# Attention on VectorE: the output addition of a pair of tiles placed apart from the sum of its last two blocks

## The reference, cut to what matters

```python
q, k, v = ...                         # 16 heads of 64, rotary embedding on q and k
scores  = einsum('bqhd,bkhd->bhqk', q, k) / 8
scores  = where(tril, scores, -1e9)   # causal
weights = softmax(scores)
out     = einsum('bhqk,bkhd->bqhd', weights, v)
x       = x + out.reshape(...) @ W_out
```

## Time and profile before

| | us |
|---|---|
| median of 3 runs (lowest, highest) | 2729.64 (2729.27, 2730.74) |
| the profiled execution, its own time | 2724.24 |
| its span in the trace | 2722.5 |
| PE busy / DVE busy / ACT busy | 2588.0 / 2075.0 / 1617.1 |
| mean granted TensorE clock, share of full speed | 0.987 |

### The profile page before, as it was taken

The page is one execution under the profiler, slowest core; times in us unless marked ns, Lnnn a source line. Parts: engine busy times, 40 slices in busy tenths (PEclk is TensorE's granted clock), DMA queues, the critical chain, the costliest instruction groups (busy, mean ns, idle before and its releaser), DMA issues. The chain is left out here.

```text
span 2722.5 us, 50823 instructions
## 1 busy us (share of the span) xinstructions
PE 2588.0 (95%) x16671; PEld 2292.4 (84%) x16671; DVE 2075.0 (76%) x4468; ACT 1617.1 (59%) x3152; POOL 1500.1 (55%) x1673
## 2 busy tenths in 40 slices
PE   7999999999999999999998799999969999999998
PEld 5888888888888888888887688888869999999997
DVE  6878888888887888887878688988856666666664
ACT  3666666666666666767666433333336666666664
POOL 3676756776656666577653444444434444444443
PEclk9999999999999999999999899999979999999999
DMA  6644454444543545453435665555344443444433
GB/s 176 121 123 117 102 136 109 117 111 118 132 103 100 134 103 125 104 123 90 106 81 124 177 180 144 159 149 142 104 136 108 105 104 56 107 108 102 106 54 47
DMA packets 192048, 316.16 MB, mean 116 GB/s; under 512 B 60048, under 2 KB 105776, under 8 KB 188784
## 3 DMA queue, kind: packets, MB, share of 16 engines
q1 hardware_dynamic: 149200, 217.90, 32.4%
q0 software_dynamic: 42656, 95.88, 14.4%
HBM read 237.41 MB, written 75.17 MB: 115 GB/s over the span
## 5 line engine op out<-in xcount | busy, mean ns | idle before, releaser
L1212 ACT ACTIVATE a_pt<-a_PT 128x512 fp32r<-128x512 f32 (+3 forms) x768 | 350.0, 490 | 390.3 <-PE a_PT L1067 384.3
L1359 DVE TENSOR_TENSOR a_pt<-a_PT,a_pt 128x512 fp32r<-128x512 f32 (+3 forms) x768 | 400.4, 548 | 117.3 <-ACT a_pt L1212 112.8
L1349 DVE CUSTOM_DVE_ANT_0 a_S<-a_S,a_mask 128x1024 f32<-128x1024 f32 (+7 forms) x512 | 386.4, 755 | 31.4 <-PE a_S L1056 30.4
L1201 ACT ACTIVATE a_pb<-a_S,a_nmax 128x1024 f32<-128x1024 f32 (+7 forms) x512 | 380.5, 743 | 40.6 <-DVE a_nmax L1349 39.3
L1067 PE MATMUL a_PT<-early_ident,a_pb 128*128 128x128 f32 x2304 | 339.6, 274 | 47.3 <-DVE a_pt L1359 43.7
L1067 PEld LDWEIGHTS a_PT<-early_ident,a_pb 128*128 128x128 f32 x2304 | 271.7, 141 | 103.6 <-issue 62.8
L1088 PE MATMUL a_O<-a_pt,a_v 128*128 128x256 f32 x2048 | 331.0, 289 | 13.9 <-DVE a_ot L1379 6.6
L1088 PEld LDWEIGHTS a_O<-a_pt,a_v 128*128 128x128 f32 x2048 | 282.0, 192 | 28.0 <-DVE a_xt L1334 11.0
L2343 POOL DMA_INDIRECT early_stage<-in_we,e_ix x116 | 130.8, 1127 | 260.0 <-issue 140.2
L1055 PE MATMUL a_S<-a_kh,a_qs 128*128 128x512 f32 (+3 forms) x768 | 270.7, 352 | 0.9 <-ACT a_pb L1201 0.9
L1056 PE MATMUL a_S<-a_kl,a_qs 128*128 128x512 f32 (+3 forms) x768 | 256.6, 346 | 0.0
(11 more groups left out here) (334 smaller groups left out, 7714.2 us busy)
## 6 DMA issues: line engine op xcount, KB each, us to landing
a_qs<-early_rot SPq DMA_DIRECT2D x256, 128.0 KB, 2.4
a_kh<-early_rot SPq DMA_DIRECT2D x256, 128.0 KB, 2.6
a_kl<-early_rot SPq DMA_DIRECT2D x256, 128.0 KB, 2.3
m_hn<-scr_hs SPq DMA_DIRECT2D x39, 516.0 KB, 3.7
scr_attT<-a_ot SPq DMA_DIRECT2D x256, 64.0 KB, 2.1
early_stage<-in_wqk POOLq DMA_DIRECT2D x31, 512.0 KB, 4.0
m_att<-scr_attT SPq DMA_DIRECT2D x30, 512.0 KB, 4.5
m_rb<-scr_rinv SPq DMA_DIRECT2D x60, 256.0 KB, 5.5
```

The source lines that it names most:

```text
L1201: act.activation(pb[u % 2][:, 0:cols], S[u % 2][:, 0:cols], ACT.Exp, bias=nmax[:, u % GU:u % GU + 1], scale=-1.0, accum_out=rsum[:, b % 2, ...
L1212: act.activation(pt[u % 2][:, 0, 4 * s:4 * s + m, (qt % 2) * P:(qt % 2 + 1) * P], PT[(k + s) % 2][:, 0:m * P].rearrange("p (k q) -> p k q" ...
L1349: dve.tensor_tensor_reduce(out=sc, in0=sc, in1=mask[:, T - cols:T], scale=-1.0, scalar=-MASKED, op0=ALU.add, op1=ALU.min, accum_out=nmax[: ...
L1359: dve.tensor_tensor(pt[u % 2][:, 1, 4 * s:4 * s + m, q], PT[(k + s) % 2][:, 0:m * P].rearrange("p (k q) -> p k q", k=m), pt[u % 2][:, 0, 4 ...
```

## The change

`out_add` is cut in two functions. `out_pair` has the wait for the value product and the sum of the last two blocks; `out_add` keeps the waits for `otmp`, for that sum and for the old store, and the output addition.

```diff
-            def out_add(k):
+            def out_pair(k):
                 dve.wait_ge(s_pv, k + 1)
                 dve.tensor_reduce(O[0:HD, 3 * P:4 * P], O[0:HD, P:3 * P].rearrange("d (a t) -> d t a", a=2), AXX,
                                   ALU.add).then_inc(s_olo, 1)
+
+            def out_add(k):
                 dve.wait_ge(s_otmp, k + 1)
                 dve.wait_ge(s_olo, k + 1)
                 if k >= 4:
...
                 k = values_turn(u - 1)
                 if k is not None and k % 2 == 0:
-                    out_add(k)
+                    out_pair(k)
                 if u == 0:
                     dve.wait_ge(s_pool, 2)
                 if u < U:
                     rowmax(u)
-                if k is not None and k % 2:
-                    out_add(k)
+                if k is not None:
+                    (out_pair if k % 2 else out_add)(k)
                 if tile_in(u, 4) is not None:
                     tile_stats(tile_in(u, 4))
                 for i, j in ends(q_steps(u - 1), 4):
                     if j < 3:
                         rope_mult(i, j)
+                if k is not None and k % 2:
+                    out_add(k)
```

## The result

The changed kernel takes 2753.29 us (median of 4 runs, 2751.67 to 2754.85), the kernel before 2730.16 (4 runs, 2729.27 to 2730.74): a ratio of 1.0088, 95% interval 1.0073 to 1.0103, so 20 to 28 us slower. Run again later beside 22 runs of the kernel before it was 1.0099 (1.0082 to 1.0116), 22 to 32 us. Forecast were 2764 us, a rise of 34.2, and a range of 2745 to 2776: the sign and the place are right, the rise is about 10 us too large.

The account below looks back on a forecast made before the run. PE's order of work was taken to bound attention. Stalls of 36.1 us, less 1.0 and 0.9, gave +34.2: 2724.24 to 2758.4 us, plus 5.4 for the runs' median, 2764 us; range 2745 to 2776.

Parts of the forecast that it names:

- The place: PE's value product waits for the output addition 60 or more times, 30 to 38 us, all in steps u % 8 = 3.
- First kind: Even pairs, mostly u % 32 = 2 and 18: odd product waits for the later addition, 0.66 us each in 33 steps.
- u = 106, 234 and 362: Steps where an input piece keeps DVE and PE already waits 1.88 us: odd product 0.25 us later in each.
- Second kind: Even pairs of u % 32 = 10 and 26, where ACT already delays the addition: 0.51 us lost in each of 26.
- Does PE get that back?: Claim that DVE's gain ends in its stops on PE soon after, so PE's lost time is not returned.
- something gives them back: Sign of error: the predicted waits at the value product are there, but attention grows by much less.
- u % 8 = 6 and the odd pairs: Even pairs there cost 0, addition 0.53 us early; odd pairs only get tile statistics ahead of the addition, -0.9 us.
- The gain in step 9: Tile statistics fill the 0.10 us gap before an odd pair's addition; in 9 of 24 steps PE waits less.
- Queues: SP's stores go 0.5 to 1.3 us later with loads behind them: 0, or at most 1 us x 31.
- The rival of the clock: New PE stops tip stretches to half clock: +27, 2791 us for 16 stops, +107, 2871 us for all 63; chance 0.08.
- Partly given back: Rival: DVE and ACT run ahead during PE's stop, half the stall is absorbed: +17, 2747 us; chance 0.14.
- The rival "faster": Earlier row maximum in 26 steps brings low halves forward, PE waits less: at most 10 us less, 2720 us; chance 0.06.

Follow-up runs that it names:

- first_kind: Kernel before, with the output addition behind the row maximum only in steps u % 16 = 2 and u % 8 = 2 of the last 32 units: 1.0075.
- after_product_late: Changed kernel, with PE's odd product in steps u % 8 = 3 behind the first half of the projection pieces: 0.9962 of the kernel before.
- second_kind: Kernel before, with the new order only in steps u % 16 = 10 outside the last 32 units, 30 steps: 1.0009.
- before_v_low_late: Kernel before, with v's low half behind the exponentials' low halves on DVE in u % 32 = 10 and 26: 0.9973.
- after_v_low_late: Changed kernel, with v's low half behind the exponentials' low halves on DVE in u % 32 = 10 and 26: 1.0092 of the kernel before.
- six_and_odd: Kernel before, with the new order only for even pairs of u % 8 = 6 and all odd pairs: 1.0008.

## Why the prediction was right, and where its size was wrong

- **The place.** Right: 62 waits at the odd product in u % 8 = 3, 33.3 us with the one in step 511 (forecast 30 to 38), none new in u % 8 = 7, and first_kind and after_product_late show that they are the loss.
- **First kind, 0.66 us x 33.** Right: 0.66 to 0.70 in the traces, +20 us (16 to 25) measured for it alone against 21.8. In u = 106, 234 and 362 the wait grew by 0.45 us, not 0.25, 0.6 us in all.
- **Second kind, 0.51 us x 26 = 13.3.** This term is mis-sized: the product is indeed 0.52 us late, but a step costs 0.19 to 0.23, about 5 us in all. The step of the prediction that failed is "Does PE get that back? ... It doesn't". I had worked out that DVE gains 0.5 us there and let it end in DVE's next stop two steps on. Between lay one more wait of PE for DVE, 0.31 us at the transpose of steps u % 32 = 11 and 27, which the gain removes: 0.52 - 0.31 = 0.21. second_kind bounds it, before_v_low_late and after_v_low_late show it. It is what the prediction named as its own sign of error, "something gives them back". These 26 x 0.31 = 8 us are most of the 10 by which the forecast was too high; the rest is within the intervals.
- **Where I could have seen it.** The list of PE's waits puts nothing there, since the gap between matmuls was small (466.63 to 466.76); the row of the weight loads has the 0.31 us, under ACT's name, 27 times in the full list of waits. I read PE's matmul rows only.
- **u % 8 = 6 and the odd pairs.** Right: six_and_odd, no measurable difference, and no rotation products stand between the two parts of an odd pair. The gain in step 9 was 0.14 to 0.19 us in nine stretches, for 0.10 forecast.
- **Queues, clock.** Next to nothing was seen of either: the scores waited 0.7 us once for a transfer, and the mean clock is 0.987 in both. The rival of the clock, beside which the Trainium skill was cited, didn't come: between 80 and 1450 us the kernel before has three stretches of 3.4 us at a granted 0.50 (at 373, 742 and 1110 us) and the changed kernel three as well (362, 755 and 1130), each close behind a wait of 1.85 to 2.32 us (a wait of 2.33 us, ended at 380 us, had none behind it); the new stops of 0.4 us brought none.
- **The rivals.** Partly given back was half right: it holds in the second kind and not in the first. The rival "faster" named a real gain, the earlier maximum, and ACT's waits did fall by 22 us, yet PE's product, which waits for the later addition, came first. after_product_late, where it doesn't wait, is faster than the kernel before.

## What to carry to other kernels

- When an operation is moved behind another on its engine, look at when the other's own input comes. In step 130 the scores were 0.36 us away from the engine's free moment: the addition was filling time in which the maximum couldn't have run, and moving it bought 0.05 us for 0.66.
- A late signal costs only if its waiter has come to it. Give the waiter work to do first and the same order gains; here the two orders had to be moved together (0.9962 against 1.0004 and 1.0099 for either alone).
- Before a stall is counted in full, follow the engine that gained by it to the waiter's next wait for it, one by one, in the rows of PE's weight loads too.

## What the runs showed of the hardware

- In steps u % 8 = 3 the first five matmuls of 128x256 of a product took 0.83 to 0.86 us when it began from a wait or right behind the addition, and 0.76 in a running stream (449.41 - 448.55 in the changed kernel; 439.32 to 440.08 in after_product_late), so such a wait of PE cost about 0.1 us more than its length. It isn't the wait alone: behind the transposes of steps u % 8 = 1 and 5 they took 0.84 us without one.
- A row maximum over 896 columns took 1.10 us when it began from a wait, 1.08 without.
- The operation behind a row maximum starts with the maximum's read-out, 0.08 us before the maximum itself ends (448.09 against 448.17), also when it is one with waits that have long been met.
- Executions of one kernel differ by up to 0.5% (2719.92 to 2733.42), while its ordinary steps repeat to 0.03 us. Between the two traces of the changed kernel the second has 2.2 us more ahead of the first scores, 5.2 us more behind the last, and 2.6 us less between them, of which 2.4 in two stretches with input pieces (units 96 to 127 and 352 to 383).
